# Stacked queries and keys written part by part from SBUF to SBUF, without the trip through a DRAM tensor

## What is computed

```python
x = _layernorm(x + _L0_attn_ref(x, ...))                 # attention 0: 16 heads of 16, rotary positions
x = _layernorm(x + _L0_xattn_ref(x, ctx, ctx, ...))      # a gated mix with decays, 8 heads of 32
x = _layernorm(x + _L0_ffn_ref(x, ...))                  # ternary weights, quantized activations
x = _layernorm(x + _L1_attn_ref(x, ...))                 # attention 1: 16 heads of 16
x = _layernorm(x + _L1_xattn_ref(x, ctx, ctx, ...))      # attention 2: queries from x, keys and values from ctx
x = _layernorm(x + _L1_ffn_ref(x, ...))

# each of the three softmax attentions, for a head of depth 16:
scores = q @ k.T * 16 ** -0.5
attn = softmax(scores)
out = attn @ v
```

## Time and profile before

| | |
|---|---|
| time before, median of 3 runs | 1619.05 us (1618.91 to 1625.47) |
| time of the profiled execution | 1622.2 us |
| its span, first to last instruction | 1620.4 us |
| mean granted TensorE clock | 0.969 of full speed |
| busy: PE, DVE, ACT, POOL | 90%, 73%, 59%, 14% |
| DMA, mean over the span | 71 GB/s |

### The profile page before, as it was taken

The page is one execution under the profiler, slowest core; times in us unless marked ns, Lnnn a source line. Parts: engine busy times, 40 slices in busy tenths (PEclk is TensorE's granted clock), DMA queues, the critical chain, the costliest instruction groups (busy, mean ns, idle before and its releaser), DMA issues. The chain is left out here.

```text
span 1620.4 us, 31692 instructions
## 1 busy us (share of the span) xinstructions
PE 1465.2 (90%) x12482; PEld 972.9 (60%) x12482; DVE 1183.2 (73%) x2103; ACT 950.7 (59%) x1701; POOL 225.4 (14%) x233
## 2 busy tenths in 40 slices
PE   7588799899999879899999888998999988898998
PEld 4155556557766556557767555565776656465577
DVE  5978887865568888974765888866565788888632
ACT  3378466674466757566355666656545586655752
POOL 6011100002221011002212210000122111100100
PEclk9699989999999999999999898999999999999999
DMA  8430113322121021521321011331322101133200
GB/s 273 139 102 2 52 47 105 118 60 79 53 69 51 2 63 48 152 67 58 119 73 53 1 47 33 93 108 50 111 72 66 53 2 46 47 97 110 70 1 26
DMA packets 115074, 114.34 MB, mean 71 GB/s; under 512 B 9842, under 2 KB 100722, under 8 KB 114930
## 3 DMA queue, kind: packets, MB, share of 16 engines
q1 hardware_dynamic: 114610, 111.28, 22.4%
q10 hardware_dynamic: 320, 1.05, 0.3%
HBM read 68.91 MB, written 42.99 MB: 69 GB/s over the span
## 5 line engine op out<-in xcount | busy, mean ns | idle before, releaser
L1170 DVE TENSOR_REDUCE nm<-psum 128x4 f16<-128x1024 f32 x384 | 455.1, 1223 | 100.3 <-PE psum L767 99.2
L1005 ACT ACTIVATE PB<-psum 128x1024 f32<-128x1024 f32 x288 | 288.3, 1024 | 87.1 <-PE psum L786 85.7
L804 PE MATMUL psum<-PB,V 128*32 128x256 f32 x2304 | 206.8, 390 | 7.4 <-ACT PB L1005 5.2
L1347 POOL TENSOR_TENSOR XO<-XO,row_b 128x512 f32<-128x512 f32 x80 | 103.2, 1300 | 749.8 <-ACT YX L976 749.8
L767 PE MATMUL psum<-QK 48*128 48x256 f16 x1536 | 140.4, 280 | 46.8 <-DVE nm L1170 22.7
L786 PE MATMUL psum<-QK 49*128 49x256 f16 x1536 | 138.3, 277 | 21.4 <-ACT PB L1005 5.3
L767 PEld LDWEIGHTS psum<-QK 48*128 48x128 f16 x1536 | 58.9, 96 | 109.8 <-DVE nm L1170 38.8
L786 PEld LDWEIGHTS psum<-QK 49*128 49x128 f16 x1536 | 54.2, 95 | 111.4 <-issue 42.1
L930 PE MATMUL psum<-YX,W 128*128 128x256 f32 x512 | 120.0, 385 | 0.0
L804 PEld LDWEIGHTS psum<-PB,V 128*32 128x32 f32 x2304 | 79.9, 110 | 62.6 <-issue 20.0
L938 PE MATMUL psum<-W,PB 128*128 128x256 f32 x512 | 116.3, 382 | 0.0
(11 more groups left out here) (171 smaller groups left out, 2675.4 us busy)
## 6 DMA issues: line engine op xcount, KB each, us to landing
QK<-heads_dram SPq DMA_DIRECT2D x96, 512.0 KB, 3.8
heads_dram<-U SPq DMA_DIRECT2D x288, 128.0 KB, 2.0
XO<-in_x SPq DMA_DIRECT2D x16, 256.0 KB, 3.2
YX<-in_ctx SPq DMA_DIRECT2D x16, 256.0 KB, 3.4
out<-XO SPq DMA_DIRECT2D x16, 256.0 KB, 2.5
W<-in_w SPq DMA_DIRECT2D x2, 1024.0 KB, 6.9
heads_dram<-PB ACTq DMA_DIRECT2D x4, 256.0 KB, 9.4
W_gu<-in_w_down SPq DMA_DIRECT2D x1, 1024.0 KB, 5.6
```

The lines of the kernel that those rows point to most:

```text
L804: ins = pe.matmul(b[SLOT * j:SLOT * j + SLOT, at:at + TOK], value(L, t, PAIRS * e + u, HEADS, HD, SLOT), src, start=(t == 0), stop=(t == T ...
L1005: act.activation(weights_of(L, unit), b[:, 0:1024], ACT.Exp, scale=HD ** -0.5)\
L1170: dve.tensor_reduce(nm[L][:, :, :, unit].rearrange("p t e -> p e t"), b[:, 0:1024].rearrange("p (e t k) -> p e t k", e=2, t=TT), AX.X, ALU ...
L1347: pool.tensor_tensor(stream(L, it), stream(L, it), row_b[:, occ:occ + 1, :].to_broadcast([P, TT, DIM]), ALU.add).then_inc(xb_ready[L], 1)
```

## The change

The DRAM tensor `heads_dram` and the step "stack" go. The step "qk" writes each part straight from `parts` in SBUF to its rows in `QS` or `KS` in SBUF. A destination of one transfer is 16 partitions of 4 KB, that is 64 KB, and its source 128 partitions of 512 bytes. So a "qk" step has four transfers for the high half (two groups by two slots) and two for the low half: 12 for each attention where there were 6 of 128 KB and 2 of 512 KB. In attentions 0 and 1 the step for K has one transfer more, two rows of ones of 4 KB from the small DRAM tensor `ones_dram`, between the high ones and the low ones. For attention 2 the row of ones is still in place. PE waits for 13, 26 and 38 transfers of a batch (`STACKED`). SP's order is the old one with the "stack" digits taken out; the orders of the other engines and the banks are the same. At the start POOL sets only one row, with one memset in place of two, and ACT issues two transfers of 4 KB in place of four of 256 KB.

```diff
-            for name in ("qk", "stack"):
-                for j in range(2 if a == 1 else 1):
-                    add(name, a, j)
+            for j in range(2 if a == 1 else 1):
+                add("qk", a, j)
...
+STACKED = (16 * 13, 16 * 26, 16 * 38)
...
-        heads_dram = [nc.dram_tensor(f"heads_dram{i}", [2, 2, 4, HD, PAIRS, TOK], F16, kind="Internal").ap()
-                      for i in range(LANES)]
+        ones_dram = nc.dram_tensor("ones_dram", [2, PAIRS, TOK], F16, kind="Internal").ap()
...
+            def stack(L, home, slot, part):
+                for k in range(KT):
+                    r = 64 * k + HD * slot
+                    sp.dma_start(home[r:r + HD, :, :], part[:, k, :]).then_inc(stacked[L], 16)
...
                 elif name == "qk":
-                    j = unit
+                    j, home = unit, (QS, KS)[unit][L]
                     sp.wait_ge(hi_ready[L], it * HI_STEPS + QK_AT[occ, unit])
                     for slot in ((0, 2) if j else (0, 1)):
-                        sp.dma_start(heads_dram[L][j, :, slot].rearrange("k r u t -> (r u) k t"), parts[L][:, 0, j])\
-                          .then_inc(part_out[j][L], 16)
+                        stack(L, home, slot, parts[L][:, 0, j])
+                    if j and occ < 2:
+                        if (it, occ) == (0, 0):
+                            sp.wait_ge(ones_out, 32)
+                        sp.dma_start(home[48:113:64, :, :], ones_dram).then_inc(stacked[L], 16)
                     sp.wait_ge(lo_ready[L], it * HI_STEPS + QK_AT[occ, unit])
-                    sp.dma_start(heads_dram[L][j, :, 1 if j else 2].rearrange("k r u t -> (r u) k t"), parts[L][:, 1, j])\
-                      .then_inc(part_out[j][L], 16)
-                elif name == "stack":
-                    if (it, occ) == (0, 0):
-                        sp.wait_ge(slots_set, 16 * LANES)
-                    sp.wait_ge(part_out[unit][L], (it * ATTN + occ + 1) * 48)
-                    sp.dma_start((KS if unit else QS)[L][:, :, :], heads_dram[L][unit].rearrange("k s r u t -> (k s r) u t"))\
-                      .then_inc(stacked[L], 16)
+                    stack(L, home, 1 if j else 2, parts[L][:, 1, j])
...
-                        pe.wait_ge(stacked[L], (it * ATTN + occ) * 32 + 32)
+                        pe.wait_ge(stacked[L], it * STACKED[-1] + STACKED[occ])
...
-            act.wait_ge(set_pool, 2)
-            load(slots_set, *[(heads_dram[L][:, :, 3].rearrange("j e r u t -> r (j e) (u t)"), last_rows) for L in range(LANES)])
-            act.wait_ge(set_pool, 4 + 2 * LANES)
+            act.wait_ge(set_pool, 1)
+            load(ones_out, *[(ones_dram[e:e + 1], preset) for e in range(2)])
+            act.wait_ge(set_pool, 3 + 2 * LANES)
...
-            setup(pool.memset(preset, 0.0))
-            pool.wait_ge(set_pool, 1)
-            setup(pool.memset(preset[0:1], 1.0))
+            setup(pool.memset(preset, 1.0))
```

More of the change, by code:

```diff
@@ L43 @@
     "loadc": "sp", "loadx": "sp", "ctx": "pe act", "xT": "pe act", "xb": "pool", "rope": "pe dve pool",
-    "qk": "pe act dve sp", "stack": "sp", "v": "pe act dve pool", "max": "pe dve", "negmax": "pe act sp",
+    "qk": "pe act dve sp", "v": "pe act dve pool", "max": "pe dve", "negmax": "pe act sp",
     "exp": "pe act", "pv": "pe act", "heads": "pe dve", "oT": "pe act", "proj": "pe dve act", "norm": "dve",
@@ L84, in attention @@
             add("qk", 2, 1)
-            add("stack", 2, 1)
             add("v", 2)
@@ L134, in lane_steps @@
     add("down1", 0, 0)
-    for name in ("qk", "stack"):
-        for j in range(2):
-            add(name, 0, j, 1)
+    for j in range(2):
+        add("qk", 0, j, 1)
     add("down1", 0, 1)
@@ L213 @@
     "sp": (
-        "4220011300002121110224443313332443000011110221223333201100011322202313233001200000312110111222223133"
-        "3333230000110111222200003332311110232221033033200001011113221102223223133332330000011112222100002113"
-        "3330112222103201333300100031111122032232221333332300001111012222003333211010132212233033231230"),
+        "4220011300212104443313244300110221332010132203123001200031211012223133332300110122003321102321030320"
+        "01011132210223231332330001122100213301221032013300103111220322321333230011012203321013212303231230"),
 }
@@ L301 @@
 C_ALL = C_FUT + P
-N_POOL = 5 + 4 * LANES
+N_POOL = 4 + 4 * LANES
 SCALED = ("r0", "r1", "r2", "mean", "inverse", "gate2", "gate2up")
@@ L386, in decoder_kernel @@
         q_k = lanes("q_k", [P, TT, 3])
-        heads_dram = [nc.dram_tensor(f"heads_dram{i}", [2, 2, 4, HD, PAIRS, TOK], F16, kind="Internal").ap()
-                      for i in range(LANES)]
+        ones_dram = nc.dram_tensor("ones_dram", [2, PAIRS, TOK], F16, kind="Internal").ap()
         psum = es.enter_context(nc.psum_tensor("psum", [P, BANKS * BANK], F32))
-        cst_loaded, qkv_loaded, rows_loaded, slots_set = (sem(n) for n in ("cst_loaded", "qkv_loaded", "rows_loaded", "slots_set"))
+        cst_loaded, qkv_loaded, rows_loaded, ones_out = (sem(n) for n in ("cst_loaded", "qkv_loaded", "rows_loaded", "ones_out"))
         raw_loaded, mask_loaded, bias_loaded, staged_in = (sem(n) for n in ("raw_loaded", "mask_loaded", "bias_loaded", "staged_in"))
@@ L399, in decoder_kernel @@
         x_loaded, c_loaded, stored = lane_sem("x_loaded"), lane_sem("c_loaded"), lane_sem("stored")
-        part_out, stacked = (lane_sem("q_out"), lane_sem("k_out")), lane_sem("stacked")
+        stacked = lane_sem("stacked")
         nm_row = lane_sem("nm_row")
@@ L433, in decoder_kernel @@
         ones_sq = flat2(XO[3][:, 1])[:, 0:P]
-        preset = flat(0, 0, 4 * TOK)[0:HD].bitcast(F16)
-        last_rows = preset.rearrange("p (a n) -> p a n", a=1).to_broadcast([HD, 4, PAIRS * TOK])
+        preset = flat(0, 0, 4 * TOK)[0:1].bitcast(F16)
         G = [flat(L, 0, 8 * TOK)[0:MH].rearrange("p (n t) -> p n t", n=8) for L in range(LANES)]
@@ L605, in weights @@
                 if unit < LANES:
-                    sp.wait_ge(stacked[unit], 32)
+                    sp.wait_ge(stacked[unit], STACKED[0])
                 if unit == 1:
@@ L1323, in _ @@
                 setup(pool.memset(V[L][:, :], 0.0))
-            pool.wait_ge(set_pool, 4 + LANES)
+            pool.wait_ge(set_pool, 3 + LANES)
             for L in range(LANES):
```

## The result

| | before | after |
|---|---|---|
| median | 1620.35 us (13 executions, 1616.32 to 1630.61) | 1628.58 us (13 executions, 1623.91 to 1636.66) |
| profiled execution's span | 1620.4 us | 1625.2 us |
| mean granted TensorE clock there | 0.969 | 0.968 |

The ratio is 1.005, with a 95% interval of 1.003 to 1.007: the kernel is 8.2 us slower by the medians. The forecast was 1615.4 us, with 1605.5 to 1626.0 as its range. The time is above the range, and it is that of the second rival (1627.9 us), SP's queue.

What follows compares the result with a forecast made beforehand. PE, busy 1465.2 of 1620.4 us, was taken as the bound. Stack waits -5.5, late rows +3.9 and the start -2.0 summed to -3.6 us, giving about 1615.4 us, range 1605.5 to 1626.

Steps and rivals of the forecast that it cites:

- second rival: SP's queue becomes the bound, rows of maxima waiting behind 13 transfers: +8.8 us, 1627.9 us at 0.65 us per issue; chance 0.18.
- (a): Issue of one transfer from 128 to 16 SBUF partitions on SP: taken as 0.50 us start to start, bounds 0.36 and 0.65.
- break-even at 0.56: Issue time in us at which 7.5 us of late rows eat the 5.5 from stack waits and 2.0 from the start.
- 13c - 5.2: Lateness of the row of maxima near 676 us, behind 13 transfers, against PE's exp start: 1.3 us at 0.50 per issue.
- 13c - 5.4: Lateness of the row of maxima near 427 us, behind 13 transfers, against PE's exp start: 1.1 us.
- three small places: Further late rows of maxima near 57.9, 78.9 and 319.1 us, put at 0.4 to 0.5 us each.
- +3.9: Cost in us of all late rows of maxima before the exp matmuls, at 0.50 us per issue.
- six stack waits: PE's waits for the stack transfer before the first max matmul, in 6 of 48 attentions: all go, -5.5 us.
- (b): Landing of one new transfer into 16 SBUF partitions: taken as 2.0 us, or 2.3 to 2.5 if such writing is slow.
- The start: First large matmul comes sooner as ACT's fills go and W_qkv's landing holds PE: -2.0 us, bounds 0 and 5.1.
- Waits only move: What PE gains at six stack waits it stands at the next DVE wait: 1621 us, no change; chance 0.15.
- More comes back: A tenth of PE's unnamed line 767 waits is the stack's, issue 0.40, start 5.1: -13.6 us, 1605.5 us; chance 0.20.

Runs made afterwards that it cites:

- m1: Changed kernel plus, after its last store, nine transfers of each of six forms on SP: issue medians some 0.6 us within SBUF, 0.43 to DRAM.
- e8: Changed kernel with one more short transfer on SP in each "qk" step, which nothing waits for: 1638.99 us, ratio 1.0095.
- e4: Kernel before with three or four short transfers to an unused DRAM tensor in each "qk" step, behind its three parts: 1669.98 us, ratio 1.0312.
- e1: Changed kernel with ACT, not SP, issuing the row of maxima in all 48 attentions, right behind its own copy: 1622.31 us, ratio 1.0008.
- w1: Changed kernel with ACT issuing the row of maxima only in the six attentions where it came late: 1616.12 us, ratio 0.997.
- e5: Changed kernel with the old start put back (second memset, four transfers of 256 KB to an unused tensor): 1633.71 us, one execution.
- v1: Changed kernel with the row of maxima issued by GpSimd instead of SP: 1633.53 us, ratio 1.0067.
- v2: Kernel before with the row of maxima issued by GpSimd instead of SP: 1636.57 us, ratio 1.0078.
- e2: Kernel before with the row of maxima issued by ACT instead of SP: 1638.40 us, ratio 1.0115.

## Why the prediction was wrong

**The step that failed is (a), the issue of one new transfer.** It was put at 0.50 us from start to start and measured 0.63 (m1: 0.59 to 0.60 of issue for five forms within SBUF). The mechanism was written down right, as the second rival, break-even at 0.56 included; the size was taken on the wrong side of it. With 0.63 the prediction's own formulas give 13c - 5.2 = 3.0 us near 680 us and 13c - 5.4 = 2.8 near 431; the trace has PE's wait up by 2.9 and 2.6. The three small places, put at 0.4 to 0.5 us each, measured 3.2 (the first exp, 5.67 for 2.42 us), 0.8 and 1.3, and one of 1.7 near 817 us was not foreseen. By the view of the waits it is +11.7 in place of +3.9, with two more of 0.2 and 0.3 us; the 1.3 is not in it, since at 320.71 us the view puts PE's wait down to DVE, though the row was issued at 318.81 and could only just have landed.

**The choice between the bounds was the error.** The row that decided against 0.65 was line 644, a transfer to DRAM. Of the rows into SBUF, those of 507 and 607 ns pointed up and the one of 332 down. Even the only one from SBUF to SBUF, 507 ns, would have given some 0.55 with the gap between two issues, still below the break-even of 0.56: no row of the trace before had the price, and only a measurement like m1 could have given it. e8 shows by dose, e4 by its row waits, and e1 and w1 by taking the row out of that queue, that the busy queue is the cause and not a companion.

**The six stack waits**: -5.5 foretold, -4.5 measured (1.0 left). A part of this was luck. The prediction had the stack near 680 us landed 8.0 us after Q's first issue; w1, where no late row hides it, has 11.4 us (673.02 to 684.43), and stack waits of 4.1 us in all. So with the rows in time the direct path gave back 1.4 us of the 5.5, and 3.1 of the 4.5 are there only because the late rows held PE up first.

**The landing (b)**: 2.0 taken; 64 KB into 16 partitions measured 2.8 in m1 at the median, most of them in a burst. Together with c it makes the stack late in w1, where the burst of ten took 6.64 us: 12 x 0.66 + 2.8 = 10.7 of the 11.4 us.

**The start**: -2.0 taken; -0.1 at the first product and +0.8 at the first max in this pair of traces, some -0.6 and -0.3 by the averages given with e5. The measured value is near the bound of 0. W_qkv took 7.8 us to land with the fills gone and 7.5 with them (6.6 to 8.1 and 7.5 to 8.1 over all traces). From 5 to 10 us the DMA engines moved 329 GB/s without the fills, as they had moved 327 with them: other loads took their place. Halving the bandwidth on paper was an estimate without a row.

**The sum with measured terms**: -4.5 + 11.7 + 0 = +7.2; the medians say +8.2, equal clock +7.0. Had only c been right (late rows 11.7) and the start 0, the forecast would have been 1619.05 - 5.5 + 11.7 = 1625.3 us, and with the measured -4.5 for the stack 1626.3. The median of the kernel before over 13 executions lies another 1.3 us higher than that of its first three, which makes 1627.6 against the measured 1628.6.

**The rivals.** "Waits only move" to DVE: refuted, 22.7 became 20.6 us. "SP's queue": this is what happened, for its own reason and near its own price (+8.8, where the measured terms give +7.2; its 13.3 for the rows was too much and its -2.0 for the start made up for it). It had a chance of 0.18, and the range was drawn to leave it out. "More comes back": refuted by the time. As for what one shifted microsecond does in a fixed order: of the 2.9 us at 687.57, 0.9 were made good by the stack wait that fell away at the next max step (0.94 before), and the other 2 stayed.

**Open**: where v1 and v2 get the smaller part of their row waits, and how far the mean clock is chance. A stack without the rows of ones, which would shorten the bursts by one, was not tried.

## What to carry to other kernels

Count the issues of a strictly ordered queue, not the bytes: eight transfers with 1.8 MB gave way to twelve with 0.8 MB, and the kernel lost 8 us, because rows of 8 KB stood behind thirteen issues of 0.63 us. When one number decides the sign and its bounds lie on both sides of break-even, measure it first: a trace that lacks the form lacks its price, and the nearest rows (0.33 to 0.61 us) do not bound the answer to one side. And move only what is late: six rows on ACT gave back 12 us by the medians (taken on different chips) and 9.1 at equal clock, all 48 gave 6 and 2.4.

## What the runs showed of the hardware that was not expected

- Issue on SP's queue in m1, medians: SBUF to SBUF 0.59 to 0.60 us, with 32 or 64 KB and with 16 or 128 partitions written; SBUF to DRAM 0.43.
- 64 KB into 16 partitions landed after 2.8 us, into 128 after 2.0 (m1, median, most in bursts).
- A row of 8 KB on a queue of its own took 5 to 6 us to land where 1.5 to 2 MB had just been issued on SP's queue (e2 at 813.69, v1 at 98.24), and 1.8 us at the median (v1).
- 48 issues of 0.52 us on ACT's queue went with 5.5 and 6.9 us more of PE's waits for ACT (e1, e2); on GpSimd's, with none (v1, v2).
- The mean granted clock moved between 0.961 and 0.975 over 44 executions of one kernel on three chips, and 0.001 of it went with 0.94 us.
